# Earlier turning of x1 and x2, normalizations ahead of gating, and the first state begun at a round's end, in a two-layer sequence kernel

## What is computed

```python
x = _layernorm(x + _L0_attn_ref(x, ...))   # state-space block
x = _layernorm(x + _L0_ffn_ref(x, ...))    # x @ sign(weight).T
x = _layernorm(x + _L1_attn_ref(x, ...))   # gated linear attention
x = _layernorm(x + _L1_ffn_ref(x, ...))    # experts, two per token
```

## Time and profile before

| what | value |
| --- | --- |
| median of 3 runs | 2445.73 us (2445.27 to 2450.8) |
| profiled execution | 2441.41 us, span 2439.5 us |
| mean granted TensorE clock | 0.949 |
| TensorE busy | 2100.3 us, 86% |
| VectorE busy | 1952.2 us, 80% |
| ScalarE busy | 1417.7 us, 58% |
| GpSimd busy | 800.3 us, 33% |

### The profile page before, as it was taken

The page is one execution under the profiler, slowest core; times in us unless marked ns, Lnnn a source line. Parts: engine busy times, 40 slices in busy tenths (PEclk is TensorE's granted clock), DMA queues, the critical chain, the costliest instruction groups (busy, mean ns, idle before and its releaser), DMA issues. The chain is left out here.

```text
span 2439.5 us, 52395 instructions
## 1 busy us (share of the span) xinstructions
PE 2100.3 (86%) x15864; PEld 1548.8 (63%) x15865; DVE 1952.2 (80%) x3681; ACT 1417.7 (58%) x3240; POOL 800.3 (33%) x1060
## 2 busy tenths in 40 slices
PE   4589989898989898989898989889889759999980
PEld 2256656575656575757565656656576659999980
DVE  6687988888888989797989798988885457777768
ACT  3466666676766666666666666666656413333334
POOL 0011415141424233242424141514142234334337
PEclk8699999999999999999999999999999979999995
DMA  6342424334232434242425152424330042222216
GB/s 176 87 114 59 116 73 98 87 82 104 65 104 65 115 79 108 66 112 66 110 59 122 47 125 61 113 71 98 91 76 21 28 154 58 58 59 58 58 56 193
DMA packets 154382, 212.88 MB, mean 87 GB/s; under 512 B 20296, under 2 KB 88912, under 8 KB 153920
## 3 DMA queue, kind: packets, MB, share of 16 engines
q1 hardware_dynamic: 132048, 144.20, 20.1%
q0 software_dynamic: 22272, 67.92, 13.6%
HBM read 134.71 MB, written 28.08 MB: 67 GB/s over the span
## 5 line engine op out<-in xcount | busy, mean ns | idle before, releaser
L1441 DVE TENSOR_TENSOR_SCAN hs<-decay,push 128x512 f32<-128x512 f32 x256 | 312.8, 1244 | 7.1
L1190 ACT ACTIVATE S<-banks,fall_tok 128x128 f32<-128x128 f32 x1024 | 278.8, 385 | 27.7 <-PE banks L823 25.4
L1011 PE MATMUL banks<-rowsT,w_here 128*128 128x128 f32 x2176 | 269.3, 277 | 7.0 <-DVE w_here L1785 6.5
L1011 PEld LDWEIGHTS banks<-rowsT,w_here 128*128 128x128 f32 x2176 | 255.6, 193 | 10.6 <-issue 9.4
L1865 POOL DMA_DIRECT2D y<-ch x96 | 88.3, 920 | 453.3 <-DVE ch L1449 351.0
L1956 POOL TENSOR_TENSOR qd<-q,q_fall 128x512 f32<-128x512 f32 x96 | 158.7, 1653 | 223.6 <-ACT chunk_fall L1175 223.6
L1549 DVE TENSOR_TENSOR S<-banks,S 128x512 f32<-128x512 f32 x256 | 167.5, 684 | 73.4 <-PE banks L835 46.9
L1997 POOL DMA_INDIRECT results_scratch<-rows_out,result_to x136 | 132.2, 972 | 240.8 <-ACT rows_out L1316 233.8
L1305 ACT ACTIVATE tanh_h<-banks 128x512 f32<-128x512 f32 x136 | 81.3, 598 | 203.7 <-PE banks L1011 169.6
L1556 DVE SCALAR_TENSOR_TENSOR oT<-tog,banks 128x512 f32<-128x512 f32 x128 | 87.3, 682 | 135.9 <-ACT sq L1158 135.8
L835 PE MATMUL banks<-q,k 64*128 64x128 f32 x1024 | 149.5, 287 | 44.0 <-DVE state L1600 29.0
(11 more groups left out here) (218 smaller groups left out, 5120.7 us busy)
## 6 DMA issues: line engine op xcount, KB each, us to landing
y<-ch POOLq DMA_DIRECT2D x96, 512.0 KB
b_all<-bc_scratch SPq DMA_DIRECT2D x128, 256.0 KB, 4.9
c_all<-bc_scratch SPq DMA_DIRECT2D x128, 256.0 KB
q_fall<-fall_scratch SPq DMA_DIRECT2D x192, 128.0 KB, 3.2
rows_in<-rows_scratch SPq DMA_DIRECT2D x136, 66.0 KB
both<-results_scratch SPq DMA_DIRECT2D x32, 256.0 KB, 3.4
w<-w_dram SPq DMA_DIRECT2D x3, 2048.0 KB, 8.9
xT<-xT_dram SPq DMA_DIRECT2D x16, 256.0 KB, 2.9
```

What stands on the lines that cost most here:

```text
L1011: mm = pe.matmul(bank_h[:, u % 2, n, here], w_here[:, u % 2, n, here], x, start=True, stop=True)
L1190: ins = nc.scalar.activation(S[:, g, here], bank[:, here], ACT.Exp, bias=fall_tok[:, head:head + 1])
L1441: nc.vector.tensor_tensor_scan(hs[:, h, :], decay[:, n % 2, h, :], push[:, h, :], 0.0, ALU.mult, ALU.add).then_inc(s_scan, 1)
```

## The change

Four edits, all of order. No arithmetic is added or taken away.

1. TensorE turns x1 in stage 5 instead of stage 6, and x2 in stage 7, ahead of `outputs(7)`, instead of at the start of the next round. ScalarE's copies go with them. x2T's place in the list of bank uses moves from the start of the round to its end, x1T's from stage 6 to stage 5, and so the banks of all other uses change.
2. VectorE normalizes x1 at the head of stage 5 and x2 at the head of stage 7, each ahead of `gate_out`.
3. ScalarE's decay 0 of the next sequence stands at the end of a round's stages, ahead of the last `squares`.
4. VectorE's first push and first two scans of the next sequence stand at the end of a round's stages, ahead of `gate_out(7)`. The product with C stays at the start of the next body.

```diff
 def ring_uses():
-    uses = [("attention", "x2T"), ("attention", "wd")]
+    uses = [("attention", "wd")]
...
-STATE_OUT = {"mix": 4, "x1T": 6, "ffn": 6}
+STATE_OUT = {"mix": 4, "x1T": 5, "ffn": 6, "x2T": 7}
...
             def stage(h, i, j, n):          # TensorE
                     if h == STATE_OUT["ffn"]:
                         sign_ffn(i)
+                    if h == STATE_OUT["x2T"]:
+                        opening(i)
...
                 if j is not None:           # TensorE, body
-                    opening(j)
                     log_decay(j)
...
             def stage(h, i, j, n):          # ScalarE
                     if h == STATE_OUT["x1T"]:
                         turn_mixed(i)
+                    if h == STATE_OUT["x2T"]:
+                        opening(i)
...
             def body(i, j, n):              # ScalarE
-                if j is not None:
-                    opening(j)
-                if i is not None:
-                    state_decay(0, i)
                 if j is not None:
                     log_decay(j)
...
                 for h in range(STAGES):
                     stage(h, i, j, n)
+                if n is not None:
+                    state_decay(0, n)
                 if j is not None:
                     squares(STAGES - 1, j)
...
             def state_scans(n, i):          # VectorE
-                if n == 0:
-                    state_part(0, 0, i)
                 state_part(n, 1, i)
                 state_part(n, 2, i)
...
             def stage(h, i, j, n):          # VectorE
                 m = STATE_IN_STAGE.get(h) if i is not None else None
+                if i is not None and h == NORM_STAGE:
+                    normalize(x1, s_rstd0, s_x1, i)
+                if i is not None and h == NORM2_STAGE:
+                    normalize(x2_new, s_rstd1, s_x2, i)
                 if j is not None:
                     if h:
                         gate_out(h - 1, j)
...
-                    if h == NORM_STAGE:
-                        normalize(x1, s_rstd0, s_x1, i)
...
-                    if h == NORM2_STAGE:
-                        normalize(x2_new, s_rstd1, s_x2, i)
...
             def body(i, j, n):              # VectorE
                 if i is not None:
-                    state_scans(0, i)
                     state_products(0, i)
...
                 for h in range(STAGES):
                     stage(h, i, j, n)
+                if n is not None:
+                    state_part(0, 0, n)
+                    state_scans(0, n)
                 if j is not None:
                     gate_out(STAGES - 1, j)
```

## The result

| what | before | after |
| --- | --- | --- |
| median of the runs | 2445.5 us (4 runs) | 2408.61 us (4 runs, 2407.13 to 2422.69) |
| ratio, 95% interval | | 0.9873 (0.9849 to 0.9897) |
| profiled execution's span | 2439.5 us | 2406.4 us |
| log_decay's first to its sixteenth product | 1736.3 us | 1705.3 us |
| a round without a fall of the clock | 115.1 us | 113.1 us |

The change makes the kernel about 1.3% faster by the ratio, 1.5% (36.9 us) by the medians; the two profiled spans are 33.1 us apart. One of the four runs took 2422.69 us, the other three 2407 to 2409. The forecast was 43.5 us, 2402 us for the median. The counts and rounds in this table are of one profiled execution each.

The account below looks back on a forecast made before the run. Neither TensorE (86% busy) nor VectorE (80%) simply bounds the kernel; time passes between them. Edits 34.5 us plus clock 9 us make 43.5 us off 2441.4, giving 2397.9, plus 4.3 for the median: 2402 us, range 2390 to 2430.

Parts of the forecast that it names:

- the waits that were to go: TensorE's waits over ten rounds: ten times 1.0 us for x_new, 0.75 us for x2T's copy, 0.68 us for x1T's copy.
- The new wait for U1_2's bank: TensorE in stage 5: x1T's turn waits 0.57 us until add_update(5) empties the bank, with outputs(5) queued behind.
- The term of the edits: Fifteen round boundaries: 1.9 us at the least, 2.6 with shorter turns, 2.3 taken; 34.5 us in all.
- project_out(3) would start at 920.02 - 2.3 = 917.7: 1.0 us of room: Round start: gate_out(7), delayed by state 0 to near 916.7, still ends 1.0 us before project_out(3) needs it.
- the three signs by which the prediction would call itself wrong: x2T copy interval above 114.5 us, VectorE waiting over 2 us for b_all, or project_out(3) waiting for sq_less.
- Does VectorE follow?: VectorE has over 3 us of room, including 2.04 us idle before residual(3), so project_out(3) stays the releaser.
- rival (4): Slower: b_all lands late and delays gate_out(7), project_out(3) and the second key product; 2461 us at 1 us a boundary, chance 0.06.
- the room takes that: Round's end: b_all, issued earlier, lands near 911.5, at worst 913.1, and the 1.0 us before project_out(3) absorbs it.
- The term of the clock: Slow products behind the x2T hole go at 7 boundaries, 1.70 us each: 12 us, counted as 9 for falls elsewhere.
- Rival (1): The low clock comes as often as before, elsewhere in the round: only 34.5 us gained, 2411 us, chance 0.14.
- x2's 1.76 us: Per boundary, TensorE's 1.01 us wait before x2T's turn and 0.75 us wait for its copy are removed.
- x1's part: Stages 5 and 6: x1's earlier normalization and turn gain net 0.1 us a boundary, up to 0.6.

Follow-up runs that it names:

- x1T_last: The changed kernel with the turn of x1 behind outputs(5) instead of ahead of it; 2404.91 us against 2447.59 before, ratio 0.9833.
- b0_first: The changed kernel with the loads of b_all and c_all for state 0 issued first in SP's body; 2397.99 us against 2447.59 before, ratio 0.9807.
- hole_filled: The kernel before with one overwritten 512-column product in TensorE's 1.01 us hole ahead of x2T's turn; 2439.03 us against 2449.55, ratio 0.9958.
- x1_alone: The kernel before with only x1 normalized ahead of gate_out(4) and turned in stage 5, banks following; 2439.10 us against 2449.55, ratio 0.9960.
- x2_alone: The kernel before with only x2 normalized ahead of gate_out(6) and turned ahead of outputs(7); 2449.70 us against 2449.55, ratio 1.0002.
- route_filled: The changed kernel with two overwritten products, ahead of the last key product and of unit 7's routing products; 2400.91 us against 2447.59 before, ratio 0.9811.
- no_state0: The changed kernel with state 0 (push, scans, decays) back at the start of a body, behind gate_out(7); 2430.34 us against 2449.55 before, ratio 0.9923.

## Why the prediction was right, and where it was not

**Right: direction, and the waits that were to go.** The measured median lies 6.6 us above the forecast and inside the range; between the profiled executions, from which the sum was made, 33 us were gained of 43.5. The three waits went. The new wait for U1_2's bank was put at 0.57 us and measured 0.50 us. x2 was ready before its turn, by 0.13 us in the round shown (1237.83 and 1237.96), and with TensorE 0.5 us earlier it is late (x1T_last). From add_ffn to log_decay's product it is 7.5 us (1233.04 to 1240.58) against 8.9 us before (905.86 to 914.80). b_all was put at a landing near the push, and the push waited 0.47 us in the round shown, 0.2 to 0.6 us where it waited at all. The step sizes took over the meeting with GpSimd's product: du takes 2.17 us where it took 1.23 us at 1019.63 in the trace of before, the 0.9 us of the forecast.

**The term of the edits: 2.3 us a boundary forecast, 2.0 us measured in a clean round.** The removed waits were sized right; what they run into was not. The step that failed is "project_out(3) would start at 920.02 - 2.3 = 917.7: 1.0 us of room". The 920.02 is from the round with the low clock, where project_out(3) comes 5.22 us behind log_decay's product. The forecast itself took away that fall in the next step, after which it comes 3.5 us behind. So the room was 1.0 - 1.7 = -0.7 us, not 1.0. In the trace project_out(3) could start at 1244.27 and starts at 1245.09. Over ten rounds it waited 0.2 to 0.9 us each time, 0.4 us on average, and it waited for sq_less: of the three signs by which the prediction would call itself wrong, this one came. It starts 3.9 to 4.6 us behind log_decay's product, not 3.5. The same slip stands at two more places. "Does VectorE follow?" counts 2.04 us to spare before residual(3), read in the same slow round; in a clean one there were 0.34, and 0.21 are left where the prediction looked for 1 us or more. And rival (4) has gate_out(7) end at 920.5 before a boundary loses 0.5 us; without the slow start that is 918.8, so it asks for a slower load than is needed.

**b_all, put at nothing: about 3 us measured.** "the room takes that" is the next step that failed, as there was no room: in the rounds where the push waits for b_all, project_out(3) comes later by as much. Over the 13 rounds it starts 2.8 us later in sum than if each began like the clean one. b0_first, where the push doesn't wait, takes this away and some 1 us more in the rounds with the cheap fall. That is rival (4)'s path, in small.

**The term of the clock: 9 us forecast, about 5 us measured.** That the seven slow starts would go was right, at all fifteen boundaries. Six costly falls came behind the routing instead, where there had been two. 9 - 6 = 3 falls of 1.7 us are 5 us. The 3 us that the forecast kept back for this were too little. Rival (1) has falls come elsewhere, but as many as before, and is 2 us off the median, in part by luck: its 34.5 us for the edits were too many by about 8. The runs show that falls move on rather than go: hole_filled and x1_alone empty the same place and fill the same other one.

**Does it add up?** 15 x 2.0 = 30 us, 5 us more from the clock, some 4 us less from b_all and the cheap falls in stage 1: 31 us, which is what the stretch from log_decay's first to its sixteenth product lost (31.0). Another 2.8 us came at the first boundary, which the prediction left out: TensorE waits there for x2 as well, and x2T's first copy moved from 106.1 to 103.3.

**Where the parts were undervalued or overvalued.** The prediction added x2's 1.76 us as if the turn ahead of outputs(7) were free. x2_alone shows that it is not: it moves the last squares back, and by itself it gains nothing. That the sum came out near is luck here: state 0's edit pays for it, which the prediction costed at nothing and described only as a risk. x1's part was put at 0.1 to 0.6 us and comes to about 0.6 us.

**Open.** What decides which weak place of the round gets the fall was not settled. The count differs between kernels whose clean rounds differ by 0.2 us, and the spread of x1T_last (2391.09 to 2409.31 us) may have the same cause, or b_all's landing; neither was tried. Also not tried: x1's and x2's early normalizations with the turn of x2 left where it was, and the wait for sq_less behind the eight products of project_out(3) that read only oT.

## What to carry to other kernels

When a wait is removed, take the spacing of all that follows, on every engine, from a round in which the removed effect is absent too; a room read from a slow round is not there any more. Moving a step ahead of another engine's last input delays everything queued behind that input, so look for work of that engine that can fill the gap, and expect the two edits to be worth something only together. In this kernel idle holes on TensorE of 0.75 to 1.5 us, two of them close together, had falls of the clock behind them that cost a further 1.7 us, and closing one handed falls to the next: count the falls of the whole round, and try a product without use in the hole.

## What the runs showed that was not expected

- A useless product made the kernel faster: about 1 us of work in a 1.01 us hole gave 10 us between the medians (hole_filled), and in the changed kernel two around the routing took away all six costly falls (route_filled).
- Rounds of one length repeat one pattern of falls. Before, 115.1 and 117.0 us alternate over eight rounds; x1_alone takes 115.9 to 116.2 us in eleven rounds in a row, with one fall at the same place in each; no_state0 has two per round, 17 and 34 us behind log_decay's product, and 116.1 us.
- A fall costs by what comes behind it: 1.7 us at the round's start and behind the routing; 0.2 to 0.5 us in stage 1, where a wait takes up most of it (none can be told in b0_first).
- A wait can move and still be worth removing: in x1T_last 0.5 us only went from one turn to the next, but VectorE's queue started earlier.
